# Expert weights of a mixture-of-experts stage, loaded in pairs of transfers that wait for each other

## The reference, cut to what matters

```python
x = x + ssm(layernorm(x))                  # scan over 2048 steps, 512 channels, 16 states
f = layernorm(x)
h = f + attention(rmsnorm(f, ln1_w))       # 16 heads
g = rmsnorm(h, ln2_w)
logits = g @ gate_w.T                      # 8 experts
rw, sel = top_k(logits, 2); rw = softmax(rw)
for e in range(8):                         # 256 -> 512 -> 256
    we = sum(where(sel == e, rw, 0), -1)
    out += (silu(g @ w1[e].T) * (g @ w3[e].T)) @ w2[e].T * we[:, None]
result = x + h + out
```

## Time and profile before

| | |
|---|---|
| timed runs, median | 3106.02 us |
| profiled execution | 3123.07 us |
| its span, first to last instruction | 3121.2 us |
| routing part (2566.9 us to the first tile load at 2704.83 us) | 137.9 us |
| tiles part (2704.83 us to the end) | 416.4 us |

### The profile page before, as it was taken

The page is one execution under the profiler, slowest core; times in us unless marked ns, Lnnn a source line. Parts: engine busy times, 40 slices in busy tenths (PEclk is TensorE's granted clock), DMA queues, the critical chain, the costliest instruction groups (busy, mean ns, idle before and its releaser), DMA issues. The chain is left out here.

```text
span 3121.2 us, 48073 instructions
## 1 busy us (share of the span) xinstructions
PE 2835.9 (91%) x14250; PEld 1220.9 (39%) x14251; DVE 2461.2 (79%) x2883; ACT 1963.7 (63%) x3570; POOL 1033.5 (33%) x507
## 2 busy tenths in 40 slices
PE   8899889899866969999999999999999987499998
PEld 3344334444322522222222222222222226499997
DVE  5999999999999668888888888888888824444443
ACT  4676665665643426888787877878788873244443
POOL 4978878879763220000000000000000003422222
PEclk9999999999999979999999999999999997699999
DMA  2111111111111542111111011111111004533332
GB/s 68 38 53 58 38 51 58 41 51 51 41 44 40 187 124 41 42 42 34 40 42 36 25 35 42 42 42 39 35 42 42 11 25 157 184 50 49 48 48 37
DMA packets 125209, 169.40 MB, mean 54 GB/s; under 512 B 25552, under 2 KB 87760, under 8 KB 125008
## 3 DMA queue, kind: packets, MB, share of 16 engines
q1 hardware_dynamic: 110992, 148.19, 16.3%
q0 software_dynamic: 13440, 18.16, 3.4%
q10 hardware_dynamic: 576, 0.55, 0.1%
HBM read 125.80 MB, written 40.74 MB: 53 GB/s over the span
## 5 line engine op out<-in xcount | busy, mean ns | idle before, releaser
L1752 DVE TENSOR_REDUCE nmh<-ring 128x2 f32<-128x1024 f32 x1024 | 1196.0, 1219 | 178.2 <-PE ring L1629 177.9
L1610 ACT ACTIVATE prob<-s_ps 128x512 f32<-128x512 f32 x2048 | 1073.0, 603 | 281.9 <-PE s_ps L1650 281.9
L413 POOL TENSOR_TENSOR bx<-u,bb 128x2048 f32<-128x2048 f32 x127 | 574.3, 4528 | 171.7 <-DVE h L889 171.7
L1650 PE MATMUL s_ps<-qs,ks 98*128 98x512 bf16 x2048 | 612.8, 387 | 17.2 <-issue 11.6
L889 DVE TENSOR_TENSOR_SCAN h<-dA,state,bx 128x512 f32<-128x512 f32 x512 | 616.5, 1264 | 11.9 <-ACT dA L674 7.8
L674 ACT ACTIVATE dA<-dt,aneg 128x512 f32<-128x512 f32 x512 | 351.5, 690 | 316.5 <-DVE h L889 311.7
L1662 PE MATMUL acc<-prob,vst 128*32 128x512 f32 x4096 | 548.8, 608 | 0.2 <-ACT prob L1610 0.2
L743 PE MATMUL y_ps<-h,ident 128*128 128x512 f32 x1024 | 476.0, 609 | 1.1 <-DVE h L896 1.1
L1650 PEld LDWEIGHTS s_ps<-qs,ks 98*128 98x128 bf16 x2048 | 149.2, 97 | 579.5 <-ACT prob L1610 478.3
L1629 PE MATMUL ring<-k,q 64*128 64x512 bf16 x2048 | 347.9, 395 | 27.8 <-DVE nmh L1752 19.6
L896 DVE TENSOR_TENSOR h<-h,c_ps 128x2048 f32<-128x2048 f32 x128 | 289.7, 2263 | 3.5 <-PE c_ps L722 3.2
(11 more groups left out here) (253 smaller groups left out, 2496.9 us busy)
## 6 DMA issues: line engine op xcount, KB each, us to landing
bb<-b_rows SPq DMA_DIRECT2D x128, 256.0 KB, 3.1
q<-parts SPq DMA_DIRECT2D x256, 64.0 KB, 2.1
parts<-part SPq DMA_DIRECT2D x48, 256.0 KB, 2.5
qs<-parts SPq DMA_DIRECT2D x192, 64.0 KB, 2.9
ks<-parts SPq DMA_DIRECT2D x192, 64.0 KB, 2.9
xt<-slots_in SPq DMA_DIRECT2D x72, 133.0 KB
k<-parts SPq DMA_DIRECT2D x256, 32.0 KB, 2.0
fo<-in_x SPq DMA_DIRECT2D x8, 512.0 KB, 4.3
```

Of the source, the lines that this page charges most:

```text
L413: nc.gpsimd.tensor_tensor(bx[:, n % BR], u[:, b], bb[:, n % RB, None, :].to_broadcast([P, KI, CH]), ALU.mult).then_inc(s_bx, 1)
L1610: nc.scalar.activation(prob[:, k % PR, j, :], s_ps[:, tile % SR, :], ACT.Exp, scale=SC).then_inc(s_exp, 1)
L1650: nc.tensor.matmul(s_ps[:, tile % SR, :], ks[:, par, hh, t * P:(t + 1) * P], qs[:, par, hh, j * CH:(j + 1) * CH], start=True, stop=True).t ...
L1752: nc.vector.tensor_reduce(nmh[:, slot, t, 2 * s:2 * s + 2], ring[:, s, :, :], AX.X, ALU.max, negate=True).then_inc(s_free[s], 1)
```

## The change

`expert_weights` now issues one matrix of one expert. The loop takes the experts two by two and the three matrices one by one, and issues the same matrix of both experts. Ahead of every pair but the first it waits until all the matrices issued so far have landed. So there are 12 pairs, of 1 MB each, with at most one pair under way. The order of the matrices changes too; bytes, places and the number of transfers don't.

```diff
-                def expert_weights(e):
-                    for dst, src in ((w1, w1T), (w3, w3T), (w2, w2T)):
-                        sp.dma_start(dst[:, e], src[e].rearrange("(k p) e -> p k e", p=P)).then_inc(s_we, 16)
+                def expert_weights(e, which):
+                    dst, src = ((w1, w1T), (w3, w3T), (w2, w2T))[which]
+                    sp.dma_start(dst[:, e], src[e].rearrange("(k p) e -> p k e", p=P)).then_inc(s_we, 16)
...
-                for e in range(NE):
-                    expert_weights(e)
+                for e in range(0, NE, 2):
+                    for which in range(3):
+                        wait(sp, s_we, 16 * 2 * (3 * (e // 2) + which))
+                        expert_weights(e, which)
+                        expert_weights(e + 1, which)
                 sp.wait_ge(s_behind, 1)
```

## The result

The change makes the kernel slower by 13 us: 3119.04 us (3116.82 to 3121.63, 5 runs) against 3106.02 us (3104.08 to 3108.34, 5 runs), ratio 1.0044, 95% interval 1.0033 to 1.0055. The forecast was 3109.0 us, 3.0 us slower, with a range up to 3117.5 us. The direction was right, the size too small by 10 us, and the time lies above the range. The profiled execution of after took 3118.43 us with a span of 3116.7 us, so it is near its timed runs, and yet 4.5 us shorter than the profile of before. That riddle turns out to be about half of the error.

What follows compares the result with a forecast made beforehand. GpSimd's scatters bound the first tile load, 2704.83 us; less 1 us gain, 2703.8. SP's new chain, 2631.42 + 11 x 6.1 + 9.25, ends at 2707.8, 3.0 us later: 3106.02 + 3.0 = 3109.0 us, range 3101 to 3117.5.

Steps and rivals of the forecast that it cites:

- What bounds before: Start of the first tile: GpSimd's 64 scatters, the last one's landing, then tile 0's load at 2704.83 us; weights off the path.
- The pile costs the routing something: GpSimd's scatters beside all weight loads at once: spreading the loads gives back 0 to 10.3 us, taken as 1 us.
- The third rival: Routing sped up without piled-up weight loads, last scatter 10.3 us earlier, rounds of 5.2 us: 3099.1 us, faster; chance 0.12.
- The price of a round, 6.1 us: SP, one pair's issue to the next: 3.9 us one transfer, 1.36 the second's bytes, 0.85 for scatters.
- Its quiet part: A pair's round on SP without scatters: 3.9 us for one transfer plus 1.36 us for the second's bytes.
- The scatters' share: Time that scatters on the DMA engines add to each pair's round: 1.17 us at most, taken as 0.85 us.
- The moved steps behind the last pair, 9.25 us: SP after the last wait: two issues 1.05, row number 1.0, zero rows 4.30, landing 2.0, tile 0's row 0.9 us.
- lies 17 us over the median of the timed runs: Profiled execution of the old kernel, 3123.07 us: its excess was taken as common, so the same 3.0 us went onto 3106.02.
- p: SP's time from one pair's issue to the next one's: bounded at 4.9 to 7.6 us, taken as 6.1 us.
- The break-even p: Time per pair on SP from which its path to the first tile load ends later than 2704.83 us: 5.83 us.
- The dearer round: Rival: a pair beside scatters takes over 6.4 us on SP; at 6.8 us 10.7 us late, 3116.7 us; chance 0.28.
- chunks 3 and 4: Sign on GpSimd: their first scatters stay 13 us apart; at 10 to 11 us the piled-up weight loads were the cause.

Runs made afterwards that it cites:

- e4_pairs_after_scatters: The changed kernel, with SP also waiting for all scatters, so every pair of weights loads behind the last scatter's landing: 3189.27 us, ratio 1.0203.

## Why the prediction was wrong

*What bounds before.* Right for the first profile and for the one without the stall: scatters, then their landing, then the tile load. On chips 1 and 11 it is SP's slow zero rows, which no row of the first profile shows.

*The pile costs the routing something, "1 us of gain, and keep 0 to 10.3".* Nothing comes back. Before without the stall has its chunks at 10.1 us with the engines at 1.05, and with the stall they are 13.3 us apart even with no weight under way (e4_pairs_after_scatters). The third rival is out; the 10.3 us that it hoped for were the stall's, as the prediction had argued from the order in time.

*The price of a round, 6.1 us.* This step failed: measured 6.7 us, a mis-sized term of the sum. Its quiet part came out, 3.9 + 1.36 = 5.26 us against 5.22, in part by luck: a single takes 3.67 us for 3.9, the second transfer 1.55 us for 1.36, and the two errors cancel. The scatters' share was 0.85 us and is 1.5: the bytes' time that I shared out was too short (2.72 us for 3.10), I took the sharing for only 0.7 of the time, and some of it stays unexplained. Eleven times 0.62 is 6.8 us.

*The moved steps behind the last pair, 9.25 us.* Measured 8.5 us without the stall (2700.59 - 2692.12), 9.0 with it. Right within 0.8 us. The weights' landing was not last, also as said.

*The sum set against the wrong execution.* The other step that failed, of about the same size, is the sentence that the profile "lies 17 us over the median of the timed runs, for a reason that is in both kernels". The reason was the stall in the routing, which both kernels can have, but it sat in the very path that the change was compared with. Two things end ahead of the first tile, scatters and SP's chain, and both start from about the same point, the free slot for the last residual rows. From there to the first tile load the profile that I used had 73.4 us (2704.83 - 2631.42), and before without the stall has 67.0. SP's chain hardly changes. So the profile showed 6.4 us of cover that the timed runs, by all that their time tells, don't have. Without it the sum with my own p reads 11 x 6.1 + 9.25 = 76.4 us against 67.0: 9.4 us slower, 3115.4 us, inside the range. With p = 6.72 and a tail of 8.5, but the old cover, it is 82.4 against 73.4, 9.0 us slower, also inside. Only both together leave the range: 82.4 us against 67.0, 15.4 us slower, and 13.0 were timed. The 12.4 us between 3.0 and 15.4 are 6.8 from the rounds and 6.4 from the cover, less 0.75 from the tail. The break-even p falls from 5.83 to (67.0 - 8.5) / 11 = 5.3 us, just over the quiet round of 5.22, so with scatters beside it no pair could have been hidden.

*The rivals.* The dearer round holds, with p = 6.7 for 6.8. That its time of 3116.7 us is near too is in part luck: it was 10.7 us over a path that the stall had made 6.4 us too long, with a tail 0.8 us too long. Its chance of 0.28 was too low since its point of decision, 6.4 us, was worked out from the stalled profile. The 8.0 us on chip 1 (5.6 by the chain), where 3.0 were forecast, do not save the sum: there before's path ends in slow zero rows, which the sum did not have.

*The signs.* Twelve pairs came, no wait for `behind`, the wait at L2041 (L2038 before) for zero rows, the chain over weights and SP, and a DMA share of 0.84 between 2634 and 2700 us for 0.8. Three did not. The last pair went at 2692.12 us and not near 2698.5, since the first was 13 us early. A p over 6.4 was named as what makes the main term wrong, and it is 6.72. And chunks 3 and 4 came at 10.1 us and not at 13, which by the prediction's own words would have made the pile the cause; the unchanged kernel without the stall shows that this sign can't tell the pile from the stall.

## What to carry to other kernels

A wait for landing behind every second transfer turns a stream into a chain of rounds. Here a round has 2.1 us fixed and 1.55 us for each 512 KB, and everything queued behind on the same engine is put off by the whole chain; a depth of two rounds gave all of that back on chip 1, with the stall (without it no such run was made). Count the rounds against the shortest cover that any run has, not against the one in the profile: where a profiled execution is longer than its timed runs by more than the effect in question, find where the extra time lies first, and if it is in the cover, take it out of the sum. And where the DMA engines are full while the stage that shares them keeps its own engine's rate (GpSimd at 1.27 us a scatter), taking load off them wins nothing.

## What the runs showed of the hardware that was not expected

- Whole sessions differ by 20 us (0.65%) for the same program: 3106 us in the first session and on chip 3, 3126 and 3129 us on chips 1 and 11. From the zero loads at L2018 to the first tile load it is 114.5 against 135.6 us, so it is in the routing part: the last scatter is issued 16 to 17 us later, and the rest is SP's zero rows at 0.70 us a step. The first profile of before has the late chunks, though not the slow zero rows, beside timed runs that are 17 us shorter. Whether it ran on the same chip as they did is not on record, and what sets the stall was not found.
- GpSimd itself is not slowed by it, nor by a full pile of loads: some 1.27 us a scatter in all.
- In all profiles of the two unchanged kernels with the stall, the chain through the routing has pieces of "another core or an unknown queue". In those without the stall it has none there.
